# Attention and feed-forward in one kernel: three first and two last units planned by hand, the first key projection by halves, and a one-input form of mean times inverse deviation

## The reference, cut to what matters

```python
x = L0_attn_x
h = (x - mean(x)) / sqrt(var(x) + 1e-5)
q, k, v = (einsum('bsd,hed->bhse', h, W) for W in (W_Q, W_K, W_V))
scores = q @ k.T / sqrt(128)            # causal: masked above the diagonal
z = softmax(scores) @ v
x = x + einsum('bhse,hde->bsd', z, W_O)
xn = layernorm(x) * gamma + beta
w_q = clip(round(weight / (mean(abs(weight)) + 1e-5)), -1, 1)
out = x + einsum('bsi,oi->bso', xn, w_q) + bias
```

## Time and profile before

| | us |
|---|---|
| median of 3 runs (lowest, highest) | 809.43 (808.97, 810.33) |
| the profiled execution | 809.58 |
| its span, first to last instruction | 807.7 |
| TensorE busy, share | 796.7, 99% |
| weight loads busy, share | 717.5, 89% |
| VectorE busy, share | 714.7, 88% |
| ScalarE busy, share | 564.7, 70% |
| GpSimd busy, share | 548.9, 68% |

### The profile page before, as it was taken

How to read it: one execution, slowest core, us unless ns; L and a number is a source line. 1 busy time by engine, 2 the same in 40 slices (tenths; PEclk the granted TensorE clock), 3 DMA queues, 4 the chain that set the end, 5 groups by cost and what they waited for, 6 DMA issues and landing times.

```text
span 807.7 us, 14732 instructions
## 1 busy us (share of the span) xinstructions
PE 796.7 (99%) x4782; PEld 717.5 (89%) x4782; DVE 714.7 (88%) x1594; ACT 564.7 (70%) x1031; POOL 548.9 (68%) x282
## 2 busy tenths in 40 slices
...
GB/s 190 85 145 159 154 162 138 117 140 145 167 147 134 135 134 153 149 148 155 136 146 119 148 158 163 141 121 131 138 170 145 150 131 121 132 147 138 125 1 106
DMA packets 57227, 111.50 MB, mean 138 GB/s; under 512 B 16960, under 2 KB 21184, under 8 KB 57152
## 3 DMA queue, kind: packets, MB, share of 16 engines
...
...
## 4 chain that ended last, share of the span: by engine, by line
PE 89%; DVE 4%; DMA 2%; SPq 2%; ACT 2%; issue 0%; ACTq 0%; DVEq 0%
PE scores L754 23%; PE ring L698 22%; PE ring L677 21%; PE ring L715 10%; PE ring L686 10%; SPq L485 2%; DMA pT<-turn 1%; PE scores L705 1%; PE ring L724 1%; ACT turn L845 1%; PE scores L744 1%; DVE scores L914 1%; DVE turn L922 1%; DMA acc<-in_x 1%; DVE stats L961 1%; DVE acc L943 1%
## 5 line engine op out<-in xcount | busy, mean ns | idle before, releaser
L563 POOL TENSOR_TENSOR pT<-pT 128x1024 fp32r<-128x1024 f32 x186 | 446.0, 2408 | 240.6 <-ACT pT L852 239.9
L845 ACT ACTIVATE turn<-scores,negmax 128x128 f32<-128x128 f32 (+7 forms) x256 | 189.8, 742 | 121.6 <-DVE negmax L914 67.3
L914 DVE CUSTOM_DVE_ANT_0 scores<-scores,mask 128x128 f32<-128x128 f32 (+7 forms) x256 | 195.2, 763 | 61.8 <-PE scores L754 60.5
L852 ACT ACTIVATE pT<-pT 128x1024 fp32r<-128x1024 f32 x186 | 196.6, 1057 | 56.1 <-DMA pT<-turn 55.5
L754 PE MATMUL scores<-kT,qT 128*128 128x512 f32 (+2 forms) x1056 | 233.0, 349 | 1.2 <-ACT turn L845 1.1
L754 PEld LDWEIGHTS scores<-kT,qT 128*128 128x128 f32 x1056 | 182.2, 188 | 27.7 <-ACT turn L845 3.2
L698 PEld LDWEIGHTS ring<-pT,v 128*128 128x128 f32 x930 | 168.1, 188 | 26.8
L698 PE MATMUL ring<-pT,v 128*128 128x512 f32 x930 | 191.6, 358 | 0.0
L922 DVE STREAM_TRANSPOSE turn<-turn 128x128 f32<-128x128 f32 (+1 forms) x248 | 181.0, 758 | 7.0 <-ACT turn L845 6.7
L715 PE MATMUL ring<-wo_s,zT 128*128 128x256 f32 x768 | 112.7, 283 | 1.5 <-DVE zT L994 1.5
L943 DVE SCALAR_TENSOR_TENSOR acc<-ring,inv,acc 128x256 f32<-128x256 f32 x256 | 111.1, 476 | 0.0
...
## 6 DMA issues: line engine op xcount, KB each, us to landing
...
```

The source lines that it names most:

```text
L563: pool.tensor_tensor(chunk(half, LO, c), f32(chunk(half, LO, c)), f32(chunk(half, HI, c)), ALU.subtract).then_inc(plo_ready, 1)
L845: act.activation(turned, columns, ACT.Exp, bias=negmax[:, t % 2:t % 2 + 1], scale=-1.0, accum_out=rowsum[:, u % 2, t:t + 1]).then_inc(prob ...
L852: act.activation(chunk(half, HI, c), f32(chunk(half, LO, c)), ACT.Copy).then_inc(phi_ready, 1)
L914: dve.tensor_tensor_reduce(out=tile, in0=tile, in1=mask[:, S - (t + 1) * P:S], scale=-1.0, scalar=FAR, op0=ALU.add, op1=ALU.min, accum_out ...
```

## The change

Three things are edited.

1. `STEADY_FROM, STEADY_TO = 3, 30`: the tables serve units 3 to 29. The start lists go on through unit 2, the end lists begin with unit 30, and both are new for all five engines. The set of items is the same.
2. The first key projection, `("qk", 2, 0)`, is done in two halves of 256 columns, each of which waits for its own xT tile.
3. Line 975, one `scalar_tensor_tensor` over all tiles with two tensor inputs (mean and rstd), becomes one `tensor_scalar` for each tile, with the mean as its only tensor input and rstd as a scalar by pointer.

The diff is cut to the lists and lines that the text speaks of; a line of "..." stands for lines left out. The lists of SyncE and the rest of the others are changed to fit.

```diff
-STEADY_FROM = 2
+STEADY_FROM, STEADY_TO = 3, 30
 START_TENSOR = (
-    ("x", 0), ("x", 1), ("warm", 30), ("qk", 2, 0), ("x", 2), ("qk", 0, 0), ("x", 3), ("qk", 0, 1), ("s", 0, 0),
-    ("qk", 2, 1), ("s", 1, 0), ("qk", 1, 0), ("qk", 3, 0), ("s", 2, 0), ("s", 3, 0), ("v", 1, -1), ("s", 4, 0),
-    ("s", 5, 0), ("x", 4), ("v", 1, 0), ("s", 6, 0), ("s", 7, 0), ("v", 0, -1), ("x", 5), ("v", 0, 0), ("s", 0, 1),
-    ("qk", 1, 1), ("s", 1, 1), ("qk", 3, 1), ("qk", 0, 2), ("x", 6), ("s", 2, 1), ("x", 7), ("s", 3, 1), ("v", 0, 1),
-    ("pv", 0, 0), ("qk", 3, 2), ("s", 4, 1), ("s", 5, 1), ("qk", 2, 2), ("s", 6, 1), ("qk", 1, 2), ("s", 7, 1),
-    ("pv", 1, 0),
+    ("x", 0), ("x", 1), ("warm", 30), ("qk", 2, 0), ("qk", 0, 0), ("x", 2), ("x", 3), ("qk", 0, 1), ("s", 0, 0),
+    ("qk", 2, 1), ("s", 1, 0), ("qk", 3, 0), ("qk", 1, 0), ("s", 2, 0), ("s", 3, 0), ("v", 1, 0), ("x", 4),
+    ("s", 4, 0), ("s", 5, 0), ("v", 1, -1), ("s", 6, 0), ("x", 5), ("s", 7, 0), ("qk", 3, 1), ("qk", 2, 2),
+    ("v", 0, 0), ("v", 0, -1), ("s", 0, 1), ("x", 6), ("s", 1, 1), ("qk", 1, 1), ("x", 7), ("qk", 0, 2), ("s", 2, 1),
+    ("s", 3, 1), ("pv", 0, 0), ("v", 1, 1), ("s", 4, 1), ("s", 5, 1), ("qk", 3, 2), ("qk", 1, 2), ("s", 6, 1),
+    ("s", 7, 1), ("qk", 1, 3), ("pv", 1, 0), ("s", 0, 2), ("s", 1, 2), ("v", 0, 2), ("o", 0, 0), ("s", 2, 2),
+    ("o", 1, 0), ("qk", 2, 3), ("s", 3, 2), ("pv", 0, 1), ("o", 3, 0), ("v", 0, 1), ("s", 4, 2), ("o", 2, 0),
+    ("qk", 0, 3), ("s", 5, 2), ("s", 6, 2), ("qk", 3, 3), ("s", 7, 2), ("pv", 1, 1),
 )
 START_SCALAR = (
...
+    ("std", 0), ("std", 1), ("norm", 0), ("norm", 1), ("x", 0), ("std", 2), ("x", 1), ("norm", 2), ("qk", 2, 0),
+    ("norm", 3), ("qk", 0, 0), ("x", 2), ("x", 3), ("qk", 0, 1), ("std", 4), ("qk", 2, 1), ("exp", 0, 0),
+    ("exp", 1, 0), ("qk", 3, 0), ("norm", 4), ("qk", 1, 0), ("exp", 2, 0), ("exp", 3, 0), ("v", 1, 0), ("x", 4),
+    ("norm", 5), ("exp", 4, 0), ("exp", 5, 0), ("v", 1, -1), ("x", 5), ("norm", 6), ("exp", 6, 0), ("qk", 3, 1),
...
 )
 END_TENSOR = (
-    ("s", 0, 31), ("s", 1, 31), ("o", 0, 29), ("v", 1, 30), ("o", 1, 29), ("s", 2, 31), ("s", 3, 31), ("pv", 0, 30),
-    ("o", 3, 29), ("o", 2, 29), ("s", 4, 31), ("tp", 0), ("tp", 1), ("tp", 2), ("s", 5, 31), ("o", 0, 30),
-    ("o", 1, 30), ("s", 6, 31), ("wsum",), ("tp", 3), ("s", 7, 31), ("tp", 4), ("tp", 5), ("pv", 1, 30), ("tp", 6),
-    ("pvl", 0), ("bw",), ("o", 3, 30), ("tp", 7), ("o", 0, 31), ("o", 2, 30), ("xf", 0), ("pvl", 1), ("o", 1, 31),
-    ("tp", 8), ("tp", 9), ("o", 2, 31), ("xf", 1), ("xf", 2), ("pvl", 2), ("xf", 3), ("o", 3, 31), ("ff", 0),
-    ("xf", 4), ("ff", 1), ("xf", 5), ("ff", 2), ("ff", 3), ("xf", 6), ("xf", 7), ("ff", 4), ("ff", 5), ("ff", 6),
-    ("ff", 7),
+    ("s", 0, 30), ("o", 0, 28), ("qk", 0, 31), ("s", 1, 30), ("o", 1, 28), ("s", 2, 30), ("pv", 0, 29), ("wsum",),
+    ("s", 3, 30), ("qk", 1, 31), ("s", 4, 30), ("qk", 2, 31), ("s", 5, 30), ("o", 3, 28), ("o", 2, 28), ("v", 1, 29),
+    ("s", 6, 30), ("o", 1, 29), ("o", 0, 29), ("s", 7, 30), ("pv", 1, 29), ("s", 0, 31), ("s", 1, 31), ("v", 0, 30),
+    ("v", 1, 30), ("qk", 3, 31), ("s", 2, 31), ("tp", 0), ("pv", 0, 30), ("tp", 1), ("s", 3, 31), ("o", 3, 29),
+    ("s", 4, 31), ("o", 2, 29), ("o", 1, 30), ("tp", 2), ("s", 5, 31), ("o", 0, 30), ("bw",), ("s", 6, 31), ("tp", 3),
+    ("s", 7, 31), ("tp", 4), ("tp", 5), ("pv", 1, 30), ("tp", 6), ("tp", 7), ("pvl", 0), ("o", 2, 30), ("tp", 8),
+    ("tp", 9), ("o", 0, 31), ("o", 1, 31), ("xf", 0), ("pvl", 1), ("o", 3, 30), ("xf", 1), ("xf", 2), ("o", 2, 31),
+    ("pvl", 2), ("xf", 3), ("ff", 0), ("o", 3, 31), ("xf", 4), ("ff", 1), ("ff", 2), ("xf", 5), ("ff", 3), ("xf", 6),
+    ("xf", 7), ("ff", 4), ("ff", 5), ("ff", 6), ("ff", 7),
 )
 END_VECTOR = (
...
+    ("edge", 1, 28), ("max", 0, 30), ("wabs",), ("pv", 1, 28), ("o", 0, 28), ("max", 1, 30), ("qk", 0, 31),
...
+    ("inv", 29), ("flip", 6, 30), ("o", 1, 29), ("flip", 7, 30), ("o", 0, 29), ("max", 0, 31), ("edge", 1, 29),
+    ("max", 1, 31), ("stat2", 0), ("pv", 1, 29), ("v", 0, 30), ("v", 1, 30), ("max", 2, 31), ("stat2", 1),
...
+    ("max", 4, 31), ("o", 2, 29), ("max", 5, 31), ("o", 1, 30), ("tp", 2), ("max", 6, 31), ("o", 0, 30), ("bw",),
+    ("stat2", 2), ("stat2", 3), ("max", 7, 31), ("tp", 3), ("tp", 4), ("tp", 5), ("edge", 1, 30), ("rstd2", 0),
+    ("inv", 31), ("pv", 1, 30), ("tp", 6), ("tp", 7), ("pvl", 0), ("o", 2, 30), ("tp", 8), ("tp", 9), ("o", 0, 31),
+    ("o", 1, 31), ("stat2", 4), ("xf", 0), ("pvl", 1), ("o", 3, 30), ("stat2", 5), ("rstd2", 4), ("xf", 1), ("xf", 2),
+    ("o", 2, 31), ("pvl", 2), ("stat2", 6), ("rstd2", 5), ("xf", 3), ("ff", 0), ("o", 3, 31), ("rstd2", 6),
+    ("stat2", 7), ("xf", 4), ("rstd2", 7), ("ff", 1), ("ff", 2), ("xf", 5), ("ff", 3), ("xf", 6), ("xf", 7),
+    ("ff", 4), ("ff", 5), ("ff", 6), ("ff", 7),
 )
 END_GPSIMD = (
-    ("lop", 0, 1, 30), ("lop", 1, 0, 30), ("lop", 1, 1, 30), ("lop", 1, 2, 30), ("lop", 1, 3, 30), ("beta",),
-    ("tern",), ("norm2", 0), ("norm2", 1), ("norm2", 2), ("norm2", 3), ("bias", 0), ("bias", 1), ("bias", 2),
+    ("lop", 0, 1, 29), ("lop", 1, 0, 29), ("lop", 1, 1, 29), ("lop", 1, 2, 29), ("lop", 1, 3, 29), ("beta",),
+    ("tern",), ("lop", 0, 0, 30), ("lop", 0, 1, 30), ("lop", 1, 0, 30), ("lop", 1, 1, 30), ("lop", 1, 2, 30),
+    ("lop", 1, 3, 30), ("norm2", 0), ("norm2", 1), ("norm2", 2), ("bias", 0), ("bias", 1), ("norm2", 3), ("bias", 2),
...
 )
...
-        for u in range(STEADY_FROM, LAST):
+        for u in range(STEADY_FROM, STEADY_TO):
...
+            def project_first_keys(dst):
+
+                for half in range(2):
+                    pe.wait_ge(job_taken, job["x", half] + 1)
+                    cols = slice(half * 2 * P, (half + 1) * 2 * P)
+                    for i, (kd, (a, m)) in enumerate([(kd, p) for kd in range(KD) for p in PASSES]):
+                        mm = pe.matmul(dst[:, cols], wk_s[:, a, kd, 0:E], xT[:, m, kd, cols], start=(half == 0 and i == 0),
+                                       stop=(i == 3 * KD - 1), skip_group_check=True)
+                return mm
...
-                    if u < 4:
+                    if (part, u) != (2, 0) and u < 4:
...
-                    mm = project_qk(part, u, dst)
+                    mm = project_qk(part, u, dst) if (part, u) != (2, 0) else project_first_keys(dst)
...
-                    dve.scalar_tensor_tensor(out=shift[:, tiles], in0=mv[:, tiles, 0], scalar=-1.0, in1=rstd[:, tiles],
-                                             op0=ALU.mult, op1=ALU.mult).then_inc(ln_step, 1)
+                    for t in range(2 * first, 2 * end):
+                        last = dve.tensor_scalar(shift[:, t:t + 1], mv[:, t, 0:1], rstd[:, t:t + 1], -1.0, ALU.mult, ALU.mult)
+                    last.then_inc(ln_step, 1)
```

More of the change, by code:

```diff
@@ L64 @@
 )
-STEADY_FROM = 2
+STEADY_FROM, STEADY_TO = 3, 30
 START_TENSOR = (
[6 rows of a table removed]
[8 rows of a table added]
 )
 START_SCALAR = (
[L77 to L84, removed]
+    ("std", 0), ("std", 1), ("norm", 0), ("norm", 1), ("x", 0), ("std", 2), ("x", 1), ("norm", 2), ("qk", 2, 0),
+    ("norm", 3), ("qk", 0, 0), ("x", 2), ("x", 3), ("qk", 0, 1), ("std", 4), ("qk", 2, 1), ("exp", 0, 0),
+    ("exp", 1, 0), ("qk", 3, 0), ("norm", 4), ("qk", 1, 0), ("exp", 2, 0), ("exp", 3, 0), ("v", 1, 0), ("x", 4),
+    ("norm", 5), ("exp", 4, 0), ("exp", 5, 0), ("v", 1, -1), ("x", 5), ("norm", 6), ("exp", 6, 0), ("qk", 3, 1),
+    ("exp", 7, 0), ("hip", 0, 0, 0), ("qk", 2, 2), ("v", 0, 0), ("norm", 7), ("v", 0, -1), ("hip", 0, 1, 0), ("x", 6),
+    ("exp", 0, 1), ("exp", 1, 1), ("qk", 1, 1), ("x", 7), ("hip", 1, 0, 0), ("exp", 2, 1), ("hip", 1, 1, 0),
+    ("exp", 3, 1), ("qk", 0, 2), ("pv", 0, 0), ("hip", 1, 2, 0), ("exp", 4, 1), ("exp", 5, 1), ("hip", 1, 3, 0),
+    ("v", 1, 1), ("qk", 3, 2), ("exp", 6, 1), ("qk", 1, 2), ("hip", 0, 0, 1), ("exp", 7, 1), ("qk", 1, 3),
+    ("hip", 0, 1, 1), ("exp", 0, 2), ("pv", 1, 0), ("v", 0, 2), ("exp", 1, 2), ("hip", 1, 0, 1), ("exp", 2, 2),
+    ("exp", 3, 2), ("qk", 2, 3), ("pv", 0, 1), ("hip", 1, 1, 1), ("hip", 1, 2, 1), ("v", 0, 1), ("exp", 4, 2),
+    ("hip", 1, 3, 1), ("exp", 5, 2), ("exp", 6, 2), ("qk", 0, 3), ("hip", 0, 0, 2), ("qk", 3, 3), ("exp", 7, 2),
+    ("hip", 0, 1, 2),
 )
@@ L87 @@
     ("clear", 0), ("stat", 0), ("stat", 1), ("rstd", 0), ("rstd", 1), ("stat", 2), ("stat", 3), ("x", 0), ("rstd", 2),
[L88 to L96, removed]
+    ("x", 1), ("stat", 4), ("stat", 5), ("qk", 2, 0), ("stat", 6), ("qk", 0, 0), ("x", 2), ("stat", 7), ("x", 3),
@@ new lines @@
+    ("max", 0, 0), ("rstd", 4), ("max", 1, 0), ("qk", 0, 1), ("qk", 2, 1), ("flip", 0, 0), ("flip", 1, 0),
+    ("qk", 3, 0), ("max", 2, 0), ("max", 3, 0), ("qk", 1, 0), ("flip", 2, 0), ("flip", 3, 0), ("max", 4, 0),
+    ("v", 1, 0), ("max", 5, 0), ("flip", 4, 0), ("x", 4), ("max", 6, 0), ("v", 1, -1), ("x", 5), ("max", 7, 0),
+    ("flip", 5, 0), ("flip", 6, 0), ("flip", 7, 0), ("qk", 3, 1), ("qk", 2, 2), ("v", 0, 0), ("max", 0, 1),
```

(20 more changed lines are left out.)

10 lines of the change are left out of this document (7 added, 3 removed), and 17 rows, old and new, of tables (END_SCALAR, END_VECTOR).

## The result

The changed kernel takes 804.31 us (median of 6 runs, 803.76 to 804.69); the kernel before, on the same chip and beside it, 808.92 us (6 runs, 808.71 to 810.33). The ratio is 0.9944, 95% interval 0.9934 to 0.9954: by the ratio 4.5 us faster, between 3.7 and 5.3.

What follows compares the result with a forecast made beforehand. TensorE was taken to bound the start and steady part, VectorE the last 30 us. Gains of 1.2 (start), 1.0 (to pv(1,30)'s edge) and 2.8 (after it) sum to 5.0 us: 804.4 us, range 802.4 to 807.8.

Steps and rivals of the forecast that it cites:

- What bounds it: Whole kernel: TensorE bounds start and steady part, VectorE the last 30 us; the start's gain passes through the steady part.
- Part 1: Start: first key projection by halves begins at about 10.2 instead of 10.65; gain 0.4 us, lower bound 0.
- Part 2: Start lists through unit 2: reordered items remove TensorE idle and spacing; 0.8 us net, bounds -0.8 and 1.6.
- Start together: Start: projection halves and new start lists together gain 1.2 us.
- Part 3: Mean times inverse deviation: one-input form avoids 1.73 us of holds behind POOL at the end, four more instructions cost 0.28.
- Part 4, checkpoint: End lists up to VectorE taking the edge of pv(1,30): 773.6 instead of 774.60, gain 1.0 us.
- No room: POOL ahead of pv(1,30): low parts ended only 0.64 us before it, TensorE comes 0.9 earlier; checkpoint taken as 773.6.
- From there: pv(1,30)'s edge to VectorE's last addition: 26.04 us busy plus 1.2 idle, 27.24 against 30.05; gain 2.8 us.
- (a): Rival, VectorE beside POOL: the one-tensor instruction is held too, 1.73 stays and 0.28 is paid; 806.4 us, chance 0.10.
- (b): Rival, start and end lists: stalls are traded, about 0.5 us at six places; 807.4 us, chance 0.18.
- (c): Rival, end: ring banks make TensorE and VectorE take turns, about 1.3 us each, seven turns; 810.9 us, chance 0.06.
- (d): Rival, join at unit 3: start's gain is lost where plan meets table; 805.6 us, chance counted within the forecast's 0.66.

Runs made afterwards that it cites:

- e3: Changed kernel with the old end lists (new start lists, halves and one-input form kept): 806.15 us, ratio to the kernel before 0.9966.
- e4: Changed kernel with the old start lists (new end lists, halves and one-input form kept): 805.44 us, ratio to the kernel before 0.9956.
- e2: Changed kernel with the first key projection in one piece, after both xT tiles: 804.33 us.
- e1: Changed kernel with the old two-input form of mean times inverse deviation: 805.57 us, ratio to the kernel before 0.9964.
- e5: Kernel before with the one-input form alone: 807.94 us against 808.60, ratio 0.9987.
- e8: Changed kernel with one idle POOL pass of 1.04 us ahead of the second low part of unit 30's half 1: 804.16 us, ratio to before 0.9942.
- e10: Changed kernel with two idle POOL passes, 2.08 us together, ahead of the second low part of unit 30's half 1: 805.51 us, ratio to before 0.9959.
- e7: Changed kernel with one one-input instruction over all tiles of a group, using the first tile's inverse deviation: 806.92 us, ratio to before 0.9977.

## Why the prediction was right

The forecast was 804.4, in 802.4 to 807.8; measured 804.31. Some of the closeness is luck with the base. The steps add up to 5.0 us off 809.43, but the kernel before ran at 808.92 beside the changed one, and the medians differ by 4.6. The profiled spans differ by 5.1 (807.7 to 802.6). Step by step:

- **What bounds it** held. The steady part carried the start's gain (e3), and e4 shows that start and end add.
- **Part 1** (0.4): start at 10.25 as said. The gain is 0.8 us in the old lists and about 0.4 in the new ones by the stages. That norm 3 comes late was seen, and cost about 0.1. Not seen: the second instruction of part 3's first pair, at 5.6 us, stands ahead of the first normalisation and puts x 1 from 7.93 to 8.11. From the first reciprocal to x 1 are 2.66 us with the new form (changed, e2) and 2.49 with the old (before, e1), whatever the input's arrival does to both. The forecast priced only the last eight of the sixteen, and the first eight stood at nothing without a reason. The last eight cost 0.90 us on VectorE and not 0.4 (17.73 to 18.72, where the old form took 0.09), but they lie beside the table load, as said.
- **Part 2** (0.8): 0.8 with the halves in, 1.25 without. Start together 1.5 (81.60 to 80.11), forecast 1.2. How the 1.5 divides between parts 1 and 2 is not settled; the sum is.
- **Part 3** (1.73 lost by holds, 0.28 for four more instructions): the holds are gone as said. The price was too low: an instruction costs 0.17 us, not 0.07, so 0.68. The threshold pair that I took it from the earlier trace rows reads PSUM and has immediate operands; the new one reads its scalar by pointer from SBUF, and which of these makes the difference was not tried. On the old end the part is worth 1.0 (e5), about what 1.73 - 0.68 gives. In the new end it is worth 2.0 (e1). The end plan was to bring 1.0 + 2.8 - 1.45 = 2.35 beside it, and brings 2.4 (e3 against the changed kernel).
- **Part 4, checkpoint** (1.0 at the edge of pv(1,30)): from unit 30's first tile to the edge it was 46.27 (774.60 - 728.33) and is 45.58 us (772.17 - 726.59), so 0.7. TensorE starts pv(1,30) 40.79 us in, 0.2 after the floor of 40.6; the 1.0 of stretched spacing in that floor was an estimate, which no row shows by itself. The waits that stay on VectorE were put at 1.3 and are 2.26 by the window. "No room" on POOL was right to 0.35 us (e8, e10).
- **From there** (27.24 us, with 26.04 busy and 1.2 idle): 27.35 (772.17 to 799.52), 26.20 busy in the window. The idle places are two of the three named: 0.50 at pv's high copy, 0.23 at the last result.

The rivals: (a), held in the new form too, is out for one element, and e7 shows it at full price for two. Its 806.4 counts the 0.28 twice, which the forecast holds already: 804.4 + 1.73 = 806.1. The argument against it by the reciprocal was weak: one tensor input did not free tensor_scalar in e7, so the reciprocal's 0.15 us did not stand for it. (b), stalls traded, is out: what new waits there are (0.51 in front of s(2,31)'s maximum, 0.50 at pv) are smaller than those removed. (c), the ring, is out: 0.9 us remain of it, at ff 3, which waits for the bank of xf 4. Its price of a turn took in a wait that is no bank's: the 1.5 us are o(3,31) waiting for the values that it reads (zT from pvl 2); only the 1.1 is a bank's. (d) is out by e3.
